# Moving sixteen more gathered tiles per round from the message table to the raw node rows, with the masks, clears and buffers that follow from it

## The reference

```
round(x, w, b): h = relu(batch_norm(x)); h = h @ w.T + b        # 5 x 128 outputs per node
                msg = h.reshape(N, 5, 128)[src, etype]; return segment_sum(msg, dst)
x = layernorm(x + round(round(x, w1, b1), w2, b2) + x)
W = ssp(ssp_in(attr)) * edge_weight                             # filter of every edge
out = segment_sum((x @ W_in)[src] * W, dst)
x = layernorm(x + ssp(out @ Wo1 + bo1) @ Wo2 + bo2)
```

## Time and profile before

| | before |
|---|---|
| median of 3 runs | 6473.5 us |
| profiled execution, own time | 6482.43 us |
| its span | 6480.6 us |
| PE busy | 4158.0 us, 64% |
| DVE busy | 3822.2 us, 59% |
| ACT busy | 1611.9 us, 25% |
| POOL busy | 4619.0 us, 71% |
| granted TensorE clock, mean | 0.727 |

### The profile page before, as it was taken

How to read it: one execution, slowest core, us unless ns; L and a number is a source line. 1 busy time by engine, 2 the same in 40 slices (tenths; PEclk the granted TensorE clock), 3 DMA queues, 4 the chain that set the end, 5 groups by cost and what they waited for, 6 DMA issues and landing times. The chain is left out here.

```text
span 6480.6 us, 66649 instructions
## 1 busy us (share of the span) xinstructions
PE 4158.0 (64%) x17271; PEld 2806.2 (43%) x17271; DVE 3822.2 (59%) x7438; ACT 1611.9 (25%) x3872; POOL 4619.0 (71%) x4787
## 2 busy tenths in 40 slices
PE   7445454544445645455454555778777889999898
PEld 4333343433334434334343444333323346666696
DVE  6544444443334777776676666544444457777698
ACT  4000000000001200000000000576666656666504
POOL 5777777777777677777777777577777777777604
PEclk9555555555556755655555676898898889999999
DMA  9211121212223521221222333333333356777696
GB/s 342 53 52 52 52 53 52 52 52 55 65 65 117 188 52 52 53 52 52 52 52 53 86 90 92 99 117 110 110 110 110 110 174 217 220 219 216 208 315 211
DMA packets 432604, 726.45 MB, mean 112 GB/s; under 512 B 104654, under 2 KB 206576, under 8 KB 431506
## 3 DMA queue, kind: packets, MB, share of 16 engines
q1 hardware_dynamic: 281652, 400.74, 19.7%
q0 software_dynamic: 150592, 321.58, 17.0%
HBM read 509.16 MB, written 212.75 MB: 111 GB/s over the span
## 5 line engine op out<-in xcount | busy, mean ns | idle before, releaser
L573 POOL DMA_INDIRECT edge_rows<-messages,idx_stage x1504 | 1446.1, 961 | 487.1 <-issue 457.9
L1658 PE MATMUL banks<-onehot,edge_rows 128*128 128x128 f32 x3008 | 715.9, 413 | 995.7 <-DMA edge_rows<-messages,idx_stage 960.8
L1658 PEld LDWEIGHTS banks<-onehot,edge_rows 128*128 128x128 f32 x3008 | 613.8, 303 | 1117.2 <-DMA edge_rows<-messages,idx_stage 1082.0
L630 POOL DMA_INDIRECT sorted_rows<-edge_rows,idx_stage x784 | 760.3, 970 | 276.3 <-issue 238.2
L630 POOL DMA_INDIRECT sorted_rows<-buf_a,idx_stage x784 | 760.5, 970 | 260.5 <-issue 241.4
L573 POOL DMA_INDIRECT buf_x<-messages,idx_stage x747 | 717.4, 960 | 227.7 <-issue 227.7
L573 POOL DMA_INDIRECT buf_a<-messages,idx_stage x747 | 714.5, 957 | 227.7 <-issue 227.7
L1040 DVE TENSOR_TENSOR buf_a<-buf_a,banks 128x128 f32 x375 | 108.1, 288 | 1044.3 <-PE banks L1658 1005.4
L689 ACT ACTIVATE h_stage<-banks,bn_shift,bn_scale 128x128 f32<-128x128 f32 x128 | 58.6, 458 | 2521.1 <-PE banks L1599 2521.1
L1658 PE MATMUL banks<-x_onehot,buf_x 128*128 128x128 f32 x1494 | 355.9, 413 | 490.6 <-DMA buf_x<-messages,idx_stage 490.5
L1658 PE MATMUL banks<-x_onehot,buf_a 128*128 128x128 f32 x1494 | 344.8, 403 | 459.9 <-DMA buf_a<-messages,idx_stage 459.5
(11 more groups left out here) (201 smaller groups left out, 7088.3 us busy)
## 6 DMA issues: line engine op xcount, KB each, us to landing
buf_a<-sorted_rows SPq DMA_DIRECT2D x593, 288.0 KB, 4.0
messages<-work SPq DMA_DIRECT2D x196, 320.0 KB
buf_a<-dst_rows SPq DMA_DIRECT2D x198, 256.0 KB
buf_a<-in_attr SPq DMA_DIRECT2D x198, 128.0 KB, 2.5
buf_a<-h_in SPq DMA_DIRECT2D x396, 64.0 KB
edge_rows<-messages,idx_stage POOLq DMA_INDIRECT x1504, 2.5
sorted_rows<-edge_rows,idx_stage POOLq DMA_INDIRECT x784
sorted_rows<-buf_a,idx_stage POOLq DMA_INDIRECT x784
```

Source lines behind the costliest of these rows:

```text
L573: nc.gpsimd.indirect_dma_start(gathered[p][h][:, t, :], None, source, bass.IndirectOffsetOnAxis(ap=idx_stage[:, h, t:t + 1], axis=0),).the ...
L630: nc.gpsimd.indirect_dma_start(sorted_rows, bass.IndirectOffsetOnAxis(ap=idx_stage[:, 2 * u + h, t:t + 1], axis=0), msg_halves[2 * u + h][ ...
L1658: last = nc.tensor.matmul(ps_sums[p][slot][j], rows_in_slot[:, j * GROUP_TILES + t, :], hot[:, j * GROUP_TILES + t, :], start=(t == 0), st ...
```

## The change

RAW_ITERS becomes (5, 5): 80 raw tiles in each round, and sixteen fewer table gathers in each pass. The pass starts at half 10, so the first table gathers go to slot 2.

To work off 80 raw tiles before iteration 74, the first 32 of them (RAW_TWICE) are taken one per half, the other 48 one per iteration. Transpose and transform of a tile now lie in the same half: the transpose before the second group, the transform behind it. DVE's three steps follow in the next half.

The clears are cut in two. In round 0 the columns 0 to 3,071 of buf_a are cleared before POOL waits for the node rows, the rest behind the raw gathers. In round 1 the columns 0 to 10,239 of buf_x are cleared directly behind gather pass 0, the rest behind the raw gathers. DVE waits for both parts.

The type masks are stored in two tensors, for types in span_bc and for the remaining columns in cut_stage, by two instructions per type instead of one; the types themselves move to x_onehot. In buf_a the message rows move from column 8192 to 10240, the attributes from 10496 to 8192 and the layer norm's sums to 12544. Since f_sb now lies under raw rows of round 1, its constant row is set by DVE before the last scale_rows and not at the start of pass 1, and SP loads the first attributes after the first chunk's x.

```diff
-MSG_COLS = 16 * 512
+MSG_COLS = 20 * 512
-RAW_ITERS = (4, 4)
+RAW_ITERS = (5, 5)
 RAW_TILES = max(RAW_ITERS) * ITER_TILES
+RAW_TWICE = 2 * 16
...
-        raw_mask = span_bc[:, 0:RAW_TILES * T].bitcast(f32).rearrange("p (n t) -> p n t", t=T)
-        raw_type = span_bc[:, RAW_TILES * T:RAW_TILES * (T + 1)].bitcast(f32)
+        masks_apart = GROUPS // T
+        raw_masks = [c.rearrange("p (n t) -> p n t", t=T) for c in (
+            span_bc[:, 0:masks_apart * T].bitcast(f32),
+            cut_stage[:, :, :].rearrange("p h t -> p (h t)")[:, 0:(RAW_TILES - masks_apart) * T])]
+        raw_type = x_onehot[:, 1, P:P + RAW_TILES]
...
-        f_sb = buf_a[0:RBF + 1, 10496:10496 + 4 * GROUP_EDGES].rearrange("p (h j n) -> p h j n", h=2, j=2)
+        f_sb = buf_a[0:RBF + 1, 16 * WIDE:16 * WIDE + 4 * GROUP_EDGES].rearrange("p (h j n) -> p h j n", h=2, j=2)
...
+        def raw_tile(p, k):
+            n = k - 2 * RAW_ITERS[p]
+            if n >= RAW_TWICE:
+                n = RAW_TWICE + (n - RAW_TWICE) // 2 if n % 2 == 0 else -1
+            return n if 0 <= n < RAW_ITERS[p] * ITER_TILES else None
+
+        def raw_half(p, k):
+            t = raw_tile(p, k)
+            return t // HALF_TILES if t is not None and t % HALF_TILES == HALF_TILES - 1 else None
...
             load_x(0)
+            sp.wait_ge(s_y, 1)
+            load_x(1)
             for h in range(2):
                 load_attributes(h, h)
-            sp.wait_ge(s_y, 1)
-            load_x(1)
             store_chunk(0)
...
             pool.wait_ge(s_short_out, 32)
+            nc.gpsimd.memset(buf_a[:, 0:6 * WIDE], 0.0).then_inc(s_clear[0], 1)
             pool.wait_ge(s_edges_in, 64)
             pool.wait_ge(s_node_out, 16 * CHUNKS)
             gather_raw(0)
-            nc.gpsimd.memset(buf_a[:, :], 0.0).then_inc(s_clear[0], 1)
+            nc.gpsimd.memset(buf_a[:, 6 * WIDE:NBUF], 0.0).then_inc(s_clear[0], 1)
             for rnd in range(2):
                 if rnd == 1:
 
+                    pool.wait_ge(s_raw_agg, 2 * RAW_ITERS[0])
+                    pool.wait_ge(s_acc[0], SUMS + 2)
+                    nc.gpsimd.memset(buf_x[:, 0:RAW_TILES * P], 0.0).then_inc(s_clear[1], 1)
                     pool.wait_ge(s_node_out, 16 * CHUNKS * 2)
                     gather_raw(1)
                     pool.wait_ge(s_closed, 2)
-                    nc.gpsimd.memset(buf_x[:, :], 0.0).then_inc(s_clear[1], 1)
+                    nc.gpsimd.memset(buf_x[:, RAW_TILES * P:NBUF], 0.0).then_inc(s_clear[1], 1)
...
                 for t in range(T):
-                    link(nc.vector.tensor_scalar(raw_mask[:, :, t], raw_type, float(t), None, ALU.is_equal))
+                    for masks, types in zip(raw_masks, (raw_type[:, 0:masks_apart], raw_type[:, masks_apart:RAW_TILES])):
+                        link(nc.vector.tensor_scalar(masks[:, :, t], types, float(t), None, ALU.is_equal))
...
             def round_pass(p):
-                dve.wait_ge(s_clear[p], 1)
-                if p == 1:
-                    nc.vector.memset(f_sb[RBF:RBF + 1, :, :, :], 1.0).then_inc(s_cut, 1)
+                dve.wait_ge(s_clear[p], 2)
...
+            nc.vector.memset(f_sb[RBF:RBF + 1, :, :, :], 1.0).then_inc(s_cut, 1)
             scale_rows(CHUNKS_IN - 1)
...
-                    if j and not beyond and 0 <= r - RAW_ITERS[p] < raw:
-                        (turn_raw, transform_raw)[h](p, r - RAW_ITERS[p])
+                    if j and raw is not None:
+                        turn_raw(p, raw)
...
-                    done = r - RAW_ITERS[p] - 1
-                    if h == 0 and HALF_TILES <= done <= raw and done % HALF_TILES == 0:
-                        sum_raw(p, done // HALF_TILES - 1)
+                    if raw is not None:
+                        transform_raw(p, raw)
+                    if raw_half(p, r * 2 + h - 2) is not None:
+                        sum_raw(p, raw_half(p, r * 2 + h - 2))
```

More of the change, by code:

```diff
@@ L94 @@
 assert ITERS % 2 == 0 and FIRST_ITERS % 2 == 0 and CHUNK_ITERS % 2 == 0
-assert all(n % 2 == 0 and (2 * HALF_TILES // 2 + 1) * n + HALF_TILES + 2 <= CHUNK_ITERS + RAW_TILES for n in RAW_ITERS)
+assert all(2 * n + 2 * n * ITER_TILES - RAW_TWICE + 4 <= 2 * CHUNK_ITERS for n in RAW_ITERS)
 assert X_COLS * X_PARTS == N and X_COLS % BN_CHUNK == 0 and GROUPS % 4 == 0
@@ L215, in gnn_program @@
         x_in, squares, centred = (work[:, i * WIDE:(i + 1) * WIDE] for i in range(3))
-        square_sum, sd, rstd = (buf_a[:, 10432 + 8 * i:10436 + 8 * i] for i in range(3))
+        square_sum, sd, rstd = (buf_a[:, NPAD + 8 * i:NPAD + 4 + 8 * i] for i in range(3))
         h_rows = buf_a[:, 8 * WIDE:9 * WIDE]
@@ L1205, in round_half @@
                             keep_places(m // 2, m % 2, m)
-                    if h == 0 and 0 <= t < raw:
+                    if t is not None:
                         pick_raw(p, t)
@@ L1215, in round_half @@
                 else:
[L1216 removed]
+                    if t is not None:
                         message_raw(p, t)
[L1218 to L1219 removed]
+                    if raw_half(p, k - 3) is not None:
+                        accumulate_raw(p, acc, raw_half(p, k - 3), (k + 1 - 2 * RAW_ITERS[p]) * 2)
                     if p == 1:
@@ L1225, in round_loop @@
                 whole = end // 2 - (end == ITERS)
-                for r2 in turns(dve, first // 2, whole, beyond):
+                for r in range(first, first + first % 2):
+                    bases = load_bases(r)
+                    for h in range(2):
+                        round_half(p, acc, r, r % 2, h, i, bases, beyond)
+                for r2 in turns(dve, (first + 1) // 2, whole, beyond):
                     for u in range(2):
@@ L1237, in hots_ahead @@
             def hots_ahead(p):
-                for half in range(1, AHEAD):
-                    build_onehot(p, 2 * RAW_ITERS[p] + half, half)
+                for half in range(2 * RAW_ITERS[p], 2 * RAW_ITERS[p] + AHEAD):
+                    build_onehot(p, half, half % GATHER_SLOTS)
             def count_beyond():
+                build_onehot(0, 2 * RAW_ITERS[0], 0)
                 raw_beyond(0, buf_a)
@@ L1687, in round_loop @@
                 whole = end // 2 - (end == ITERS)
-                for r2 in turns(pe, first // 2, whole, beyond):
+                for r in range(first, first + first % 2):
+                    for h in range(2):
+                        aggregate(p, r // 2, r % 2, h, beyond)
+                for r2 in turns(pe, (first + 1) // 2, whole, beyond):
                     for u in range(2):
```

58 lines of the change are left out of this document (28 added, 30 removed).

## The result

The changed kernel is slower by 0.3%: 6494.6 us median (6491.7 to 6498.0, 8 runs) against 6473.9 us (6469.2 to 6477.1, 8 runs), a ratio of 1.0034 with a 95% interval of 1.0025 to 1.0042. Measured again later it was 6496.7 against 6478.1 us, 1.0029 [1.0018, 1.0040]. The prediction was 6438.5 us, with 0.03 for slower; the loss is about 20 us where a gain of 35 was forecast.

The account below looks back on a forecast made before the run. POOL, issuing gathers without a gap, was taken to bound both gather passes. Gains of 15.3 us (round 0) and 20.2 us (round 1) less 0.5 us (end of pass 1) gave 35.0 us, 6473.5 to 6438.5 us; range 6432 to 6451.

Parts of the forecast that it names:

- Gathers taken from the passes: Both gather passes: 16 fewer table gathers at 1.264 us each take 20.2 us off each pass.
- Raw work once per half: First 32 halves of a pass: added vector and PE work fits idle time and the 21.5 us lead; costs nothing.
- Start of pass 0: Before pass 0: added raw gathers and the clear's rest move the first table gather from 164.42 to 169.3, giving back 4.9 us.
- Start of pass 1: Before pass 1: added raw gathers and remaining clear stay hidden; POOL still waits 4.4 us for the message table.
- End of pass 1: Before the last scale_rows: the moved 1.76 us memset of f_sb exceeds 1.20 us idle; 0.5 us lost.
- Convolution unchanged: After pass 1: moved attribute loads and buffer columns cost nothing, so the convolution keeps its length.
- What that clear runs beside: Between the rounds: the clear behind pass 0 holds an index copy but not its successors; taken as zero, upper bound 8.0 us.
- The first rival: Between the rounds: the clear stops the vector engine, all 8.0 us pass on, giving 6446.5 us; chance 0.29.
- Message stores delayed: Before pass 1: added raw gathers delay the message stores by 2.9 us, giving 6441.4 us; chance 0.10.
- three signs of being wrong: Early gathers released by index copies; last message store later after its block; convolution length changed by over a few microseconds.
- The vector engine falls behind in the dense stretch: First 32 halves of a pass: vector lag exceeds its 21.5 us lead, making the kernel slower, 6498 us; chance 0.03.
- The change does nothing: Whole kernel: what POOL gives up returns as waits elsewhere, 22 us or more; chance 0.05.

Follow-up runs that it names:

- m1: Kernel of its own, not the reference: gathers, then clears, beside chosen vector instructions; gathers 0.944 us median beside nothing, nearly all 1.57 beside two-SBUF multiplies alternating with sums.
- e1c: Changed kernel with the raw tile's bias result kept in PSUM, so the mask multiply reads one SBUF operand; faster level: 6463.6 us, 0.9983 of the kernel before.
- a0: The changed kernel again, unaltered, at the faster level: 6496.7 us, 1.0029 of the kernel before.
- e6c: Changed kernel with a copy of 384 PSUM columns ahead of each mask multiply, at the faster level: 6465.8 us, 0.9983 of the kernel before.
- e1: Changed kernel with the raw tile's bias result kept in PSUM; first run, at the slower level: 7864.8 us, 1.0007 of the kernel before.

## Why the prediction was wrong

*What bounds the kernel* was right: GpSimd issues gathers through both passes without a gap, before and after.

*Gathers taken from the passes, 20.2 us each*: right as a count, wrong as a sum. The step that failed is "Raw work once per half ... No gather waits ... The sum at this place is nothing". It looked for gathers that start late, only in the 32 halves in a row, and priced a gather at a constant 1.264 us. No gather started late; they became longer, by 25 us a pass, beside the multiply whose row I had used for the vector engine's load alone. More than half of that, 35.5 of 58.6 us in the two passes, came with the 48 tiles behind those halves, of which that step says nothing. The rows of before held a hint: 5.3 us of lengthening with L1140 in pass 0, which a mean of 961 ns hides. The Trainium skill (SBUF — State Buffer, "Who interferes with whom") says that a vector instruction with two SBUF inputs contends with a GpSimd instruction that reads SBUF, and not with one that only writes. The traces agree with both halves: 1.57 us for gathers beside such a multiply, 7.44 us for ten multiplies beside a clear. The same section infers that the descriptor work of a gather does not meet such an instruction; here it does, by up to 0.64 us in m1.

*Start of pass 0*, 4.9 us given back: 4.0; the clear ended 0.8 us before the index copies were there. *Start of pass 1*, the raw gathers and the second clear hidden: right. *End of pass 1*, 0.5 us: 0.2. *Convolution unchanged*: within 2 us.

*What that clear runs beside*: "I take zero" was the wrong end. The first rival, with 0.29, gave 8.0 us; the statistics came 5.8 us late and pass 1 7.2 to 8.1. The prediction quotes "fully blocked" and sets it aside; the copy was blocked for 7.99 us. The instruction behind the copy began 0.07 us after it in both cases. After a hold of 0.4 us it ended on time, being 1.22 us long itself; in the hold of 8 us it did not end before the clear. I had read a short hold as a rule for a long one.

*Message stores delayed*: in small part. The raw gathers still end before the table has landed, as the prediction said, but the table lands some 1.1 us later behind its last block, 4.80 us for 3.65, where this rival gave 2.9; that is one of the three signs of being wrong that the prediction lists, and nothing tells whether the added gathers do it. *The vector engine falls behind in the dense stretch*: not in the changed kernel; in e1c it did, by a wait of PE that the edit brought. *The change does nothing*: the time came near it, by a way that it did not name. None of the prediction's three signs of being wrong looks at the length of a gather.

Against the forecast column of the table the spans differ by -0.9 + 20.5 + 7.2 + 20.8 - 0.3 - 2.0 = 45.3 us, rounded row by row; the spans are 6490.8 and 6445.6, 45.2 apart. The medians miss by 56.1, since the profiled execution of before lay above its median and that of after below it.

## What to carry to other kernels

When one engine's instruction rate is the bound, price what runs beside it by operands and by place: a vector instruction of 128x640 that reads two SBUF tiles can add up to 0.64 us to a gather that it meets, a long copy within SBUF adds too, and a schedule that repeats every 8 gathers repeats the meeting. One operand in PSUM takes it away; check then what waits for the PSUM that is held longer. Half a microsecond of other work ahead of it took it from 30.3 to 6.0 us in one pass and only from 29.2 to 19.1 in the other, so look at the trace after. Where an edit moves an instruction of one engine, look also for the instructions of another that wait for it: they are moved too. Don't leave copies without a reader next to a long clear on GpSimd.

## What was not expected of the hardware

An indirect gather waits for a two-SBUF instruction that began before it and is still under way about 0.11 us after its start, and then ends 0.82 us after that instruction's end (1.58 us for an end at 0.76); the copy L1116 ends so too. In the trace of the changed kernel all 146 mask multiplies that began 0.04 us or more before a gather and ended 0.11 us or more into it did so. The two that ended within its first 0.06 us did not, nor the one that began only 0.01 us before it, nor any of the 6 that began in its first 0.13 us. A bf16 addition of 392 columns does it too, but ends soon: 1.12 us at most in m1. A copy held by a clear lets three instructions behind it begin, none of which ends before the clear does; the traces of a0, e1c and e6c show the same as that of after (7.92 to 7.97 us for the copy). And there are two levels of time: the same kernel takes 6,474 to 6,478 us at one and 7,844 to 7,912 at the other, and one edit (e1) stands at 0.9983 of the kernel before at the first, at 1.0007 and 1.0042 at the second.
